# An audio tower in five overlapped parts: other orders of the stages within a turn

## What is computed

```python
h = L0_tok(x)                       # depthwise conv of 7 taps, 192x192 matmul, relu, max-pool by 2 (62 tokens),
                                    # real part of a 2-D DFT, normalisation with gamma and beta
h = h + L0_attn(layernorm(h))       # 8 heads, relative positions (a second score matrix, skewed by rows)
h = h + L0_ffn(layernorm(h))        # ternary weights, activations rounded to 8 bits, silu gate, width 512
h = h + L1_attn(layernorm(h))       # 12 query heads, 3 key and value heads, rotary
h = h + L1_ffn(layernorm(h))        # router picks 1 of 8 experts for each token, silu gate, width 512
```

## Time and profile before

| what | value |
|---|---|
| median of three runs | 1188.11 us |
| profiled execution, its own time | 1188.7 us |
| its span | 1186.9 us |
| TensorE busy | 1003.6 us (85%) |
| ScalarE busy | 836.7 us (70%) |
| VectorE busy | 791.9 us (67%) |
| GpSimd busy | 363.1 us (31%) |
| tile phase | from 0 to about 1000 us |
| expert phase | the remaining 187 us |

### The profile page before, as it was taken

The page is one execution under the profiler, slowest core; times in us unless marked ns, Lnnn a source line. Parts: engine busy times, 40 slices in busy tenths (PEclk is TensorE's granted clock), DMA queues, the critical chain, the costliest instruction groups (busy, mean ns, idle before and its releaser), DMA issues. The chain is left out here.

```text
span 1186.9 us, 31215 instructions
## 1 busy us (share of the span) xinstructions
PE 1003.6 (85%) x9406; PEld 760.6 (64%) x9439; DVE 791.9 (67%) x2641; ACT 836.7 (70%) x2673; POOL 363.1 (31%) x1096
## 2 busy tenths in 40 slices
PE   3748889998999999989899989999998653999996
PEld 2626666666666666666666666666665432888885
DVE  2346777777777777777777777777776433555553
ACT  2437888888888888888888888888887531333332
POOL 2112333333333333333333333333333211122222
PEclk9878999999999999999999999999999755999999
DMA  6153111111111111111111111111112203122221
GB/s 220 34 179 99 34 40 39 45 39 39 39 41 54 43 45 43 39 39 39 39 39 45 39 39 39 39 56 39 47 40 78 69 7 127 50 59 57 57 59 42
DMA packets 74256, 65.62 MB, mean 55 GB/s; under 512 B 39342, under 2 KB 63697, under 8 KB 74097
## 3 DMA queue, kind: packets, MB, share of 16 engines
q1 hardware_dynamic: 64832, 49.58, 14.2%
q0 software_dynamic: 3680, 9.38, 2.2%
q10 hardware_dynamic: 5712, 6.29, 1.9%
HBM read 36.57 MB, written 28.95 MB: 55 GB/s over the span
## 5 line engine op out<-in xcount | busy, mean ns | idle before, releaser
L1207 DVE SCALAR_TENSOR_TENSOR conv_lo<-xT_lo,c_taps,conv_lo 128x248 f32<-128x248 f32 x192 | 89.9, 468 | 14.9 <-ACT xT_hi L910 14.9
L1152 ACT ACTIVATE e_tanh<-bank_a 128x512 f32<-128x512 f32 x34 | 20.3, 597 | 104.7 <-PE bank_a L593 104.7
L1102 ACT ACTIVATE p<-bank_b,max 128x62 f32<-128x62 f32 x384 | 81.4, 352 | 0.0
L501 POOL TENSOR_TENSOR var_y<-ssq_y,c_eps 128x1 f32<-128x1 f32 x32 | 6.1, 189 | 235.4 <-ACT f_sq L1072 235.4
L593 PE MATMUL bank_a<-e_xT,w_now 128*128 128x128 f32 x544 | 70.5, 284 | 5.8 <-DVE e_gate L1484 1.5
L593 PEld LDWEIGHTS bank_a<-e_xT,w_now 128*128 128x128 f32 x544 | 64.9, 196 | 15.1 <-issue 12.1
L593 PE MATMUL bank_a<-c_wv,a_xT 64*64 64x384 f32 (+1 forms) x512 | 74.0, 503 | 0.0
L593 PE MATMUL bank_a<-a_xT,c_wq 64*128 64x128 f32 (+1 forms) x512 | 71.7, 282 | 0.0
L593 PE MATMUL bank_a<-c_wo,oT 128*128 128x192 f32 x384 | 68.5, 328 | 0.4 <-ACT oT L910 0.4
L593 PE MATMUL bank_a<-a_xT,c_wk 64*128 64x128 f32 (+1 forms) x512 | 68.8, 280 | 0.0
L593 PEld LDWEIGHTS bank_a<-a_xT,c_wq 64*128 64x128 f32 (+1 forms) x512 | 64.3, 191 | 4.3 <-ACT a_xT L910 0.4
(11 more groups left out here) (262 smaller groups left out, 3006.6 us busy)
## 6 DMA issues: line engine op xcount, KB each, us to landing
rel_scores<-rel_tok SPq DMA_DIRECT2D x32, 492.0 KB, 2.6
rel_skew<-rel_scores SPq DMA_DIRECT2D x64, 124.0 KB, 3.1
x_tok<-in_x SPq DMA_DIRECT2D x32, 187.5 KB
e_rest<-routed SPq DMA_DIRECT2D x34, 97.0 KB, 1.9
e_tok<-routed SPq DMA_DIRECT2D x34, 96.0 KB, 1.9
routed<-pad_rows SPq DMA_DIRECT2D x8, 386.0 KB, 3.5
w_sb<-in_w ACTq DMA_DIRECT2D x1, 3072.0 KB, 12.2
w_sb<-in_w ACTq DMA_DIRECT2D x2, 1024.0 KB, 14.2
```

The source lines that it names most:

```text
L501: pool.tensor_tensor(out=var[k][:, :], in0=ssq[k][:, :], in1=c_eps[:, width:width + 1], op=ALU.mult).then_inc(var_eps[k], 1)
L1102: last = nc.scalar.activation(p1[:, h, 0:T], src[:, at * T:(at + 1) * T], ACT.Exp, bias=max1[:, mx:mx + 1])
L1152: nc.scalar.activation(e_tanh[:, :], pa0[:, :], ACT.Tanh, scale=0.5).then_inc(e_tanhr, 1)
L1207: c.mark(v.scalar_tensor_tensor(conv_lo[:, :, :], xT_lo[:, :, k:k + PAIRS], c_taps[:, 0, k:k + 1], conv_lo[:, :, :], ALU.mult, ALU.add))
```

## The change

Only the five tables are new: the order of the stages on TensorE, ScalarE, VectorE and GpSimd, and for many stages the number `late`. SyncE's table and every stage stay the same. Of the tables, the first lines for ScalarE and for VectorE:

```diff
@@ ScalarE @@
-                (2, a_copy_x), (1, t_middle_tap), (1, t_copy_x), (4, b_normalise_in), (3, f_normalise_in),
+                (3, a_copy_probs), (4, f_round_x), (4, f_copy_x), (5, b_copy_q), (1, t_middle_tap),
+                (2, a_normalise_in), (4, f_tanh_gate), (3, a_copy_heads_hi), (2, a_copy_x), (1, t_copy_x),
...
@@ VectorE @@
-                (5, b_residual), (4, f_residual), (3, a_residual), (1, t_convolve_1), (2, a_bias_q),
+                (5, b_rotate), (2, t_norm), (3, a_normalise), (5, b_key_blocks), (4, f_silu), (5, b_max_scores),
```

More of the change, by code:

```diff
@@ L565, in _ @@
             overlapped(pool, (
-                (4, f_dequant_x), (3, a_keep), (4, f_inv_sqrt_y), (2, t_inv_sqrt), (2, t_scale), (6, r_scatter),
-                (4, f_dequant_y), (4, f_scale), (3, a_scale), (3, f_inv_sqrt_x), (5, b_scale)))
+                (2, t_scale), (4, f_inv_sqrt_y), (4, f_dequant_y), (5, b_scale), (4, f_scale), (3, a_scale),
+                (2, a_keep), (3, f_inv_sqrt_x), (5, r_scatter), (3, f_dequant_x), (1, t_inv_sqrt)))
             def mark_weights(landed, es):
@@ L866, in _ @@
             overlapped(pe, (
[L867 to L872, removed]
+                (4, f_transpose_x), (5, b_transpose_qk), (1, t_transpose), (4, f_project_up), (4, f_project_gate),
+                (3, a_transpose_heads), (2, a_transpose), (5, b_scores), (2, a_project), (3, a_output),
+                (5, b_probs_transpose), (2, a_relative), (5, b_values), (4, f_transpose_y), (5, b_transpose_o),
+                (4, f_down), (5, b_output), (2, a_project_v), (1, t_pointwise), (5, r_transpose), (2, a_scores),
+                (5, r_route), (2, a_add_relative), (1, t_dft), (4, b_transpose), (5, r_rank), (1, t_dft_seq),
+                (4, b_project), (2, a_probs_transpose), (2, a_values)))
             def e_transpose(j):
@@ L1129, in _ @@
             overlapped(act, (
-                (2, a_copy_x), (1, t_middle_tap), (1, t_copy_x), (4, b_normalise_in), (3, f_normalise_in),
[L1131 to L1136, removed]
+                (3, a_copy_probs), (4, f_round_x), (4, f_copy_x), (5, b_copy_q), (1, t_middle_tap),
+                (2, a_normalise_in), (4, f_tanh_gate), (3, a_copy_heads_hi), (2, a_copy_x), (1, t_copy_x),
+                (3, a_copy_heads_lo), (4, f_square_y), (5, b_expo), (2, a_copy_k), (5, b_copy_probs), (4, f_round_y),
+                (2, a_copy_rel_even), (2, a_copy_rel_odd), (4, f_copy_y), (5, b_copy_o), (2, a_bias_qw),
+                (2, a_copy_v0), (5, r_keep), (5, r_normalise_in), (5, r_copy_x), (1, t_relu), (2, a_copy_v1),
+                (4, b_normalise_in), (3, f_normalise_in), (5, r_expo), (3, f_square_x), (1, t_copy_z), (4, b_copy_x),
+                (2, a_expo), (4, b_copy_v)))
             def e_copy_x(j):
@@ L1436, in _ @@
             overlapped(dve, (
-                (5, b_residual), (4, f_residual), (3, a_residual), (1, t_convolve_1), (2, a_bias_q),
-                (1, t_convolve_2), (4, b_rotate), (3, f_quantise_x), (4, b_key_blocks), (1, t_pool),
-                (4, b_max_scores), (3, f_silu), (5, r_choose), (5, r_choose_one), (2, a_max_scores), (1, t_moments),
-                (3, f_quantise_y), (1, t_norm), (4, b_normalise), (2, a_normalise), (5, r_slots)))
+                (5, b_rotate), (2, t_norm), (3, a_normalise), (5, b_key_blocks), (4, f_silu), (5, b_max_scores),
+                (1, t_convolve_1), (2, a_bias_q), (4, f_quantise_y), (5, b_normalise), (1, t_convolve_2),
+                (5, b_residual), (4, f_residual), (3, a_residual), (1, t_pool), (5, r_choose), (5, r_choose_one),
+                (2, a_max_scores), (5, r_slots), (3, f_quantise_x), (1, t_moments)))
             n_plan = [n_setup[0]]
```

## The result

| | before | after |
|---|---|---|
| median of the runs, us | 1187.98 (1187.19 to 1189.46, 4 runs) | 1219.62 (1216.48 to 1223.37, 4 runs) |
| ratio of after to before | | 1.0264, 95% interval 1.0247 to 1.0281 |
| profiled execution, time and span, us | 1188.7, 1186.9 | 1220.0, 1218.2 |

A forecast was written before the change was run, and what follows sets the result against it. A ring of handovers between ScalarE and TensorE bounds the turn: 15.98 + 11.62 + 0.6 + 0.3 + 0.2 = 28.7 us. 28 x 0.94 = 26.3, ends +1, on 1188.7 gives 1216, median 1215; range 1186 to 1238.

The forecast's parts named there:

- The turn: Time from one `a_values` to the next in the steady stretch: 28.7 us, 0.94 more than the 27.76 before.
- ScalarE's legs: ScalarE's stretches of the closed chain, priced from the rows before the change: together 15.98 us a turn.
- the step through `t_copy_z`: From TensorE's `t_dft` to ScalarE's `t_copy_z` and back to `t_dft_seq`: 0.42 plus two handovers, 0.6 us.
- Handovers: Passing work between engines costs 0.06 us each; five besides those of `t_copy_z`, 0.3 us a turn.
- legs 3 and 4: ScalarE from `t_middle_tap` to `b_copy_o`, then TensorE from `b_output` to `b_project` with a step to `t_copy_z`.
- The small wait before `b_copy_probs`: ScalarE arrives 0.2 us early for a transpose TensorE reaches only behind `a_project` and `a_output`; 0.2 in the sum.
- the second rival: ScalarE's stages start closer together, 0.94 or more missing; new order wins, turn 26.7, time 1159 us; chance 0.16.
- the ring: Longest chain through ScalarE and TensorE closing one turn later: 28.4 to 29.0 us, time 1207 to 1224; chance 0.60.
- The waits: TensorE stands still 4.2 us a turn, before 2.3; ScalarE waits 1.8 before `a_copy_v0`, 0.8 before `r_copy_x`.
- The start: `a_values` tile 0 to 1, 40.8 us before: 8 off, since ScalarE's weight-load issue and f's ternary weights delay less.
- the third case of the prediction: `rel_tok` copies' trip to `a_add_relative` (or `a_normalise`) comes late; if 0.5, turn 29.2, time 1229 us; chance 0.18.
- The end: `a_values` of tile 31 to its scatter: 81 us against 72.2, 9 more, three whole turns to go; bounds 0 and 15.

The follow-up runs named there:

- The repeats in legs 3 and 4: Changed kernel with one more ScalarE bank copy ahead of `b_copy_probs`, 1285.38 us; separately, changed kernel with `b_output`'s matmuls made twice, 1245.27 us.
- the filler: `b_transpose_o`'s two transposes made three times instead of once, added to the changed kernel with the extra bank copy ahead of `b_copy_probs`: 1234.66 us.
- the repeats ahead of a wait: Changed kernel with one more bank copy in front of `a_copy_heads_lo`, 1226.32 us; separately, changed kernel with `a_probs_transpose`'s four transposes made twice, 1226.61 us.
- the first experiment: Changed kernel with one ScalarE copy of a full bank made once more into a spare tile, ahead of `b_copy_probs`: 1285.38 us, turn 30.72 us.

## Why the prediction was right, point by point

**The time.** 1219.62 against 1215. On the profiled executions it is 1220.0 against 1216, and the 4.0 are: turns -1.5, start +7.4, end -2.5, experts +0.6. So the turns carried the prediction, and the two ends missed by more than the total shows.

**The turn: right, and in the main for its reason.** 28.65 against 28.7, 28 turns worth +24.8 against 26.3. That the sum of 28 comes this close has some luck in it: one fall of the clock added 1.63 and the last turn was 1.27 shorter than that of before; the prediction had neither. The kinds of parts can be compared. ScalarE's legs measure 2.49 + 13.46 = 15.95 with the wait in them, against 15.98 + 0.2. TensorE's measure 1.41 + 10.98 = 12.39 with the step through `t_copy_z`, against 11.62 + 0.6. Handovers: 0.31 for four, against 0.3 for five. The errors, -0.23 and +0.17, nearly cancel, which is luck. The step from `t_dft` over `t_copy_z` to `t_dft_seq` is 630.94 - 630.48 = 0.46, not 0.6, so TensorE's stages took 11.93, not 11.62. The repeats in legs 3 and 4 show that time added there is added to the turn (+0.48 with the clock kept up by the filler, and +0.65), and the repeats ahead of a wait cost 0.00 and 0.10.

**The small wait before `b_copy_probs`: mis-sized.** "ScalarE arrives 0.2 early" was 0.53. The sum hardly noticed, since ScalarE's stages by themselves took 15.95 - 0.53 = 15.42 and not 15.98, and the two errors cancel: luck again. In the new order the stages do start closer together than in the rows of before, as the second rival had it, but by 0.56 and not by the 0.94 that it needed. And it means that the ring does not stay on ScalarE through all of leg 3: between `a_copy_x` and `b_copy_probs` it runs over TensorE's `a_project`, `a_output` and `b_probs_transpose`, and ScalarE has half a us free there. The copy repeated in front of `a_copy_heads_lo` shows that: 0.50 more of work, and no change of the turn.

**The waits.** TensorE: 1.1 before `a_values` (1.3 written), 0.8 before `f_down` (1.0), 0.5 before `f_transpose_y` (0.6), 0.6 before `a_transpose` (0.55). The wait before `b_project` is gone. ScalarE waits 2.2 for `a_project_v` (1.8) and 0.7 before `r_copy_x` (0.8). In the regular turns there is no wait for `rel_skew`, and none of TensorE before `a_project`, `a_relative` or `t_dft_seq` that the timeline lists, where I had 0.2 to 0.3 each. The prediction's list of waits did not fit its own turn: 25.1 of work and 4.2 of waits are 29.3, not 28.7; measured are 2.9 in the four waits above and 28.65 - 25.4 = 3.2 of idle time. Busy time: TensorE 25.4 where I said unchanged at 25.1, ScalarE 23.3 where I said 24.0; the sum over the ring has neither as a term.

**The start: the sum was mis-sized.** I took 8 off and it was 0.6. ScalarE's stop while it issues weight loads stayed in front of `t_copy_z`:

```profile
82.65 0.33 ACT L910 ACTIVATE z_sb<-bank_t 128x192 f32<-128x192 f32 x1 [10.34 <-issue]
```

From tile 0 to tile 1 it is 34.3 instead of 40.8, a gain of 6.5. But tile 0 came 3.8 later, and tiles 1 to 3 took 2.2 more. Among the waits of TensorE in these first turns are three for the skewed scores, one for each of tiles 0, 1 and 2:

```profile
47.01 1.10 PE L593 MATMUL bank_a<-rel_skew,ident 128*128 128x496 f32 x2 [2.31 <-DMA rel_skew<-rel_scores]
...
72.37 1.37 PE L593 MATMUL bank_a<-rel_skew,ident 128*128 128x496 f32 x2 [1.87 <-DMA rel_skew<-rel_scores]
...
109.19 1.10 PE L593 MATMUL bank_a<-rel_skew,ident 128*128 128x496 f32 x2 [1.90 <-DMA rel_skew<-rel_scores]
```

The kernel before has one such wait there, of 0.69 us, for tile 0. So the way over the transfer, the third case of the prediction, did hold TensorE up in the first turns. The step from tile 1 to tile 2 is 30.86 where it was 29.20, and the wait of 1.90 for tile 2 is more than that difference. Tile 0 comes later for another reason too: its copies of `rel_tok` start at 38.80, 2.6 later than before. `t_transpose` of tile 1 now stands ahead of `a_transpose` of tile 0 and stops 3.40 for its load; with that load early the copies start at 38.86, but there the cast of the f weights came 2.2 later, so whether this wait alone delays them stays open. I had followed the two causes in the rows of before, and not what the new order puts in front of tile 0, nor the transfer in turns that are not yet regular. What the three waits for `rel_skew` cost together was not tested.

**The end: right in sign.** +6.5 against +9.

**The rivals.** Behind the one that ends faster stands a rule of the Trainium skill ("Perfetto Trace Analysis", Identifying the Most-Contended Engine): optimise the engine that is busiest first. Here that is ScalarE. By the trace, ScalarE's share of the stretch fell from 87% to 81% while the time rose; a copy added to it cost nothing in one place, 0.29 in another and, with the clock kept up, 0.48 in a third. The trace does not agree with that reading here: the place decided, not the load. The longer ring over `rel_skew` held TensorE up only in the first turns of the changed kernel; the run with one copy behind `b_copy_o` shows how near it was in the others: with `rel_tok` complete 0.95 us later, TensorE waits for it in 13 of 20 turns.

**What stays open.** In the changed kernel the clock fell in one turn of 28 with the same rows ahead of it as in the others. What singled that turn out, no row shows. The four times of after spread over 6.9 us, those of before over 2.3; a few falls more or less at 1.63 would do that, but I saw the clock of one execution only in the detail needed.

## What to carry to other kernels

When no engine is full and every turn is alike to a hundredth, lay one turn out as a ring of handovers and add its legs; an order moves the ring, not the sums. Before you trust a leg, ask of each stage on it what stands in front of it on its own engine, for that is where two of my misses came from (`b_copy_q` behind `a_values`, and what stands in front of tile 0). Look at the first turns by themselves: three waits for a transfer that no regular turn has stood there. And a wait can cost more than its length: in the first experiment the clock fell behind such waits turn after turn, and transposes that nobody needs were the repair.

## What I had not expected of the hardware

TensorE's granted clock fell to 0.50 (1.2 GHz) for some 3.3 us right behind a stretch in which it had worked 2.02 of 3.70 us, in 27 turns running of one kernel, and each fall cost about 1.6 us; in the kernel with 2.46 of 3.70 there it fell in none of the turns between tiles 3 and 31, and in the one with 2.22 of 3.50 in one of 28. A copy of 0.5 us thus cost 2.1 a turn, 66 us in all, of which 54 lie in the 28 turns, and 0.45 us of useless work a turn took 50.7 of the 66 back.
